# Handing the token-shifted input of the feed-forward to transfers alone, without the staging copies on GpSimd

## The reference

```python
def shift_tokens(t):
    a, s = jnp.split(t, 2, -1)
    s = jnp.pad(s, ((0, 0), (1, 0), (0, 0)))[:, :-1]
    return jnp.concatenate([a, s], -1)

for i in range(DEPTH):          # DEPTH = 6
    x = attn_layer(shift_tokens(x), Wqkv[i], q_scale[i], k_scale[i], Wo[i]) + x
    x = ffn_layer(shift_tokens(x), ln_g[i], ln_b[i], W1[i], b1[i], W2[i], b2[i]) + x
```

## Time and profile before

| | |
|---|---|
| runs of the kernel before | 6000.32, 6006.6 and 6016.27 us (median 6006.6) |
| the profiled execution | 6016.27 us, its span 6014.3 us |
| mean granted TensorE clock | 0.957 of full speed |
| PE, DVE, ACT, POOL busy | 91%, 72%, 68%, 46% of the span |
| `xs` by DMA from `staged` | 24 times, 254 KB and 1.8 KB |
| `w_qk` loads | 196 of 128 KB, median 2.1 us from issue to landing |

### The profile page before, as it was taken

One profiled execution on the slowest core, in us unless ns is written; L12 is line 12 of the kernel. 1 busy time (PEld: TensorE's weight loads), 2 busy tenths in 40 slices (PEclk: granted clock), 3 DMA queues, 4 the chain that ended last, 5 costly groups with the idle time before them and its releaser, 6 DMA issues. The chain is left out here.

```text
span 6014.3 us, 154805 instructions
## 1 busy us (share of the span) xinstructions
PE 5498.8 (91%) x57658; PEld 3896.3 (65%) x57658; DVE 4315.4 (72%) x6698; ACT 4082.8 (68%) x7766; POOL 2765.6 (46%) x2459
## 2 busy tenths in 40 slices
PE   8887996799999999999997888799999999999997
PEld 3223332677777777777776322677777778777775
DVE  7875645677777777777775886777777777777774
ACT  5774654577777777777774577577777777777774
POOL 1101100565656665556663110666556566555662
PEclk8997997899999999999999899899999999999998
DMA  0000000100000000000000000100000000000000
GB/s 12 1 1 5 2 1 9 32 18 15 18 16 15 22 15 21 14 19 16 17 20 10 4 1 1 35 16 17 18 14 19 17 16 22 14 18 16 16 20 16
DMA packets 128105, 87.16 MB, mean 14 GB/s; under 512 B 32596, under 2 KB 121200, under 8 KB 127320
## 3 DMA queue, kind: packets, MB, share of 16 engines
q1 hardware_dynamic: 127320, 76.74, 4.5%
HBM read 68.96 MB, written 1.05 MB: 12 GB/s over the span
## 5 line engine op out<-in xcount | busy, mean ns | idle before, releaser
L1742 POOL TENSOR_TENSOR cross<-raw,tab_b 128x512 f32<-128x512 f32 x768 | 999.2, 1325 | 291.7 <-ACT raw L1612 288.8
L732 DVE TENSOR_REDUCE arena<-PS 128x1 f32<-128x512 f32 (+3 forms) x1408 | 837.6, 648 | 252.5 <-PE PS L550 162.1
L1748 POOL CAST kT_b<-kT 128x512 bf16<-128x512 f32 x384 | 300.0, 781 | 1317.5 <-ACT kT L1666 1317.5
L683 ACT ACTIVATE arena<-PS 128x1024 f32<-128x1024 f32 (+1 forms) x704 | 656.4, 968 | 324.0 <-PE PS L573 238.5
L1841 DVE TENSOR_TENSOR oT<-PS,rec_den 128x288 f32<-128x288 f32 (+1 forms) x768 | 326.4, 425 | 637.2 <-ACT rec_den L1646 637.2
L1812 DVE TENSOR_TENSOR rot<-PS,tab_a 128x512 f32<-128x512 f32 x768 | 522.5, 686 | 233.0 <-PE PS L1491 142.7
L1460 PE MATMUL PS<-qT,kT 64*128 64x96 f32 x8448 | 659.3, 286 | 0.0
L1612 ACT COPY raw<-PS 128x512 f32<-128x512 f32 x768 | 448.0, 591 | 287.7 <-PE PS L1491 247.3
L1638 ACT ACTIVATE PT<-PS 128x576 f32<-128x576 f32 (+1 forms) x768 | 468.9, 611 | 254.3 <-PE PS L1460 243.3
L1828 DVE TENSOR_TENSOR rot<-rot,cross 128x1024 f32<-128x1024 f32 x384 | 611.7, 1593 | 13.3 <-POOL cross L1742 11.3
L550 PE MATMUL PS<-k_parts,q_parts 32*128 32x512 f32 (+3 forms) x1408 | 505.4, 509 | 92.7 <-DVE arena L732 78.3
(11 more groups left out here) (255 smaller groups left out, 12972.2 us busy)
## 6 DMA issues: line engine op xcount, KB each, us to landing
w_qk<-in_w_pairs SPq DMA_DIRECT2D x196, 128.0 KB, 2.1
w_v<-in_w_pairs SPq DMA_DIRECT2D x100, 128.0 KB, 2.2
w_o<-in_w_out_pairs SPq DMA_DIRECT2D x192, 64.0 KB, 1.8
xs<-staged SPq DMA_DIRECT2D x24, 254.0 KB
w<-in_L_ffn_W SPq DMA_DIRECT2D x12, 341.0 KB
q_parts<-max_rows SPq DMA_DIRECT2D x192, 2.0 KB
raw<-in_c_E SPq DMA_DIRECT2D x2, 896.0 KB, 4.5
w<-in_L_ffn_W SPq DMA_DIRECT2D x24, 64.0 KB
```

The source lines that it names most:

```text
L683: nc.scalar.activation(PT[u % 4].rearrange("p (a n) -> p a n", a=2)[:, :, first_q:512], PS[:, 2 * (u % 2):2 * (u % 2) + 2, first_q:512], A ...
L732: nc.vector.tensor_reduce(maxima[:, 2 * m + h, qt, kh:kh + 1], bank[:, 0:keys_of(qt, kh)], AX.X, ALU.max).then_inc(bank_free, 1)
L1742: nc.gpsimd.tensor_tensor(dst[:, :, :, o:o + 32], src[:, :, :, other:other + 32], tab[:, :, o:o + 32].unsqueeze(2).broadcast_to([128, 8, 2 ...
```

## The change

The POOL copies and the `staged` tile go. `xs` becomes one tile [128, 8, 128]. SP itself now waits for the two additions to x and issues three DMAs that read `x_tok` directly: the unmoved half (128 partitions, 8 pieces of 64 floats each), the moved half (127 partitions, 8 pieces of 64 floats each), and the row that wraps (7 pieces). A piece is 256 bytes. The semaphore `staged_in` goes; POOL's bias addition now waits for `xs_in`, that is, for the landing of all three. DVE reads a tile of `xs` as 128 adjacent floats instead of two runs of 64.

```diff
--- before.py
+++ after.py
@@ -1153,7 +1153,7 @@
         rec_den = [own(f"rec_den{m}", [128, 3 * QC]) for m in range(2)]
         base_a, base_b, tab_a, tab_b = (own(name, [128, BT, 128]) for name in ("base_a", "base_b", "tab_a", "tab_b"))
         scales, swapped = own("scales", [128, 128]), own("swapped", [128, 128])
-        xs, staged = own("xs", [128, 2, BT, C // 2]), own("staged", [128, BT, C // 2])
+        xs = own("xs", [128, BT, C])
         n_parts = [own(f"n_{name}", [128, N], F32R) for name in ("high", "low")]
         gated = [own(f"gated{n}", [128, N]) for n in range(3)]
         w1, w2 = own("w1", [128, 2 * INNER]), own("w2", [128, 3, C])
@@ -1195,7 +1195,7 @@
                     for z in (kT[m], qT[m], kT_b[m], qT_b[m], max_parts[m]):
                         nc.gpsimd.memset(z[:, :], 0.0).then_inc(zeroed, 1)
                 nc.gpsimd.memset(R[:, :, :], 0.0).then_inc(zeroed, 1)
-                nc.gpsimd.memset(xs[:, :, :, :], 0.0)
+                nc.gpsimd.memset(xs[:, :, :], 0.0)
                 nc.gpsimd.memset(floors[:, 0:1], -1e-24)
                 nc.gpsimd.memset(floors[:, 1:2], 65536e-24)
 
@@ -1333,11 +1333,11 @@
         with stage("full", "free0", "free1", "free2", "free3", "max_turned", "rows_made", "wqk_in", "wqk_split", "wv_in", "wv_split", "wo_in", "scales_in", "tab_a_made", "tab_b_made",
                    "st_full", "exp_done", "pv_full", "ln_done", "den_done", "o_done",
                    "raw_in", "sq_done", "red_done", "bounded", "ln2_done", "rn_ready", "cross_done", "add_done", "rot_done", "cast_done",
-                   "ff_in", "w1_split", "staged_in", "xs_in", "b2_added", "stat", "lnv", "rs", "normed", "nl_done", "xh_in", "passed") as (
+                   "ff_in", "w1_split", "xs_in", "b2_added", "stat", "lnv", "rs", "normed", "nl_done", "xh_in", "passed") as (
                 block, full, free0, free1, free2, free3, max_turned, rows_made, wqk_in, wqk_split, wv_in, wv_split, wo_in, scales_in, tab_a_made, tab_b_made,
                 st_full, exp_done, pv_full, ln_done, den_done, o_done,
                 raw_in, sq_done, red_done, bounded, ln2_done, rn_ready, cross_done, add_done, rot_done, cast_done,
-                ff_in, w1_split, staged_in, xs_in, b2_added, stat, lnv, rs, normed, nl_done, xh_in, passed):
+                ff_in, w1_split, xs_in, b2_added, stat, lnv, rs, normed, nl_done, xh_in, passed):
             free = (free0, free1, free2, free3)
 
             def filled(eng, l, b, p, name):
@@ -1392,9 +1392,12 @@
                             src = I["w_out_pairs"][bass.ds(l * PAIRS + (p - 1 + m), 1), :, :]
                             sp.dma_start(w_o[m][:, :], src.rearrange("o p n -> (o p) n")).then_inc(wo_in, 16)
                     if ff and p == 1:
-                        need(sp, staged_in, ff_index(l, b) * 2 + 2)
-                        sp.dma_start(xs[1:128, 1, :, :], staged[0:127, :, :]).then_inc(xs_in, 16)
-                        sp.dma_start(xs[0:1, 1, 1:BT, :], staged[127:128, 0:BT - 1, :]).then_inc(xs_in, 16)
+                        taken_apart(sp, l, b, 1, "Y0")
+                        taken(sp, l, b, 1, "Y1")
+                        src = x_tok[:, BT * (1 - b):BT * (1 - b) + BT, :]
+                        sp.dma_start(xs[:, :, 0:64], src[:, :, 0:64]).then_inc(xs_in, 16)
+                        sp.dma_start(xs[1:128, :, 64:128], src[0:127, :, 64:128]).then_inc(xs_in, 16)
+                        sp.dma_start(xs[0:1, 1:BT, 64:128], src[127:128, 0:BT - 1, 64:128]).then_inc(xs_in, 16)
                     if a:
                         if b == 1 and p == 1:
                             need(sp, tab_a_made, l + 1)
@@ -1763,12 +1766,6 @@
                         cross_terms(l, b, p, 1)
                         need(pool, full, fill(l, b, p, "Q3") + 1)
                         split_qk(it + 1)
-                    if ff and p == 1:
-                        taken_apart(pool, l, b, 1, "Y0")
-                        taken_apart(pool, l, b, 1, "Y1")
-                        src = x_tok[:, BT * (1 - b):BT * (1 - b) + BT, :]
-                        nc.gpsimd.tensor_copy(xs[:, 0, :, :], src[:, :, 0:64]).then_inc(staged_in, 1)
-                        nc.gpsimd.tensor_copy(staged[:, :, :], src[:, :, 64:128]).then_inc(staged_in, 1)
                     if a:
                         cast(l, b, p, 0)
                         cast(l, b, p, 1)
@@ -1788,7 +1785,7 @@
                         nc.gpsimd.tensor_tensor(w1_parts[1][:, :], w1[:, :], w1_parts[0][:, :], ALU.subtract).then_inc(w1_split, 1)
                     if ff and p == 2:
                         need(pool, ff_in, (l + b) * 96)
-                        need(pool, staged_in, phi * 2 + 2)
+                        need(pool, xs_in, phi * 48 + 48)
                         x = x_tok[:, BT * (1 - b):BT * (1 - b) + BT, :]
                         nc.gpsimd.tensor_tensor(x, x, b2_row[:, :].unsqueeze(1).broadcast_to([128, BT, C]), ALU.add).then_inc(b2_added, 1)
 
@@ -1848,9 +1845,9 @@
                 def late(l, b, p, slot):
                     phi, ff = ff_index(l, b), present(l, b, p)[4]
                     if ff and p == 2 and slot == 2:
-                        need(dve, xs_in, phi * 32 + 32)
+                        need(dve, xs_in, phi * 48 + 48)
                         for t in range(BT):
-                            nc.vector.bn_stats(stats[:, t, :], xs[:, :, t, :]).then_inc(stat, 1)
+                            nc.vector.bn_stats(stats[:, t, :], xs[:, t, :]).then_inc(stat, 1)
                     if ff and p == 2 and slot == 3:
                         need_apart(dve, stat, phi * 16 + 8)
                         for t in range(BT):
@@ -1858,7 +1855,7 @@
                     if ff and p == 3 and slot in (1, 2):
                         need(dve, rs, phi + 1)
                         for t in range(4 * slot - 4, 4 * slot):
-                            nc.vector.tensor_scalar(normed_tok[:, t, :].rearrange("p (h e) -> p h e", h=2), xs[:, :, t, :], moments[:, t, 0:1], rstd[:, t:t + 1],
+                            nc.vector.tensor_scalar(normed_tok[:, t, :], xs[:, t, :], moments[:, t, 0:1], rstd[:, t:t + 1],
                                                     ALU.subtract, ALU.mult).then_inc(normed, 1)
                     for name in late_names(l, b, p, slot):
                         kind, f = name[0], int(name[1])
```

## The result

The changed kernel takes 6053.74 us in the median (6048.82 to 6063.87, 4 runs) against 6004.14 (6000.32 to 6016.27, 4 runs): ratio 1.0085, 95% interval 1.0067 to 1.0101, about 50 us slower. The direction and the path of the loss were forecast, the size was not: 103 us were forecast, twice as much.

A forecast was written before the change was run, and what follows sets the result against it. PE, busy 91%, was taken as the bound, so stalls count only if they reach it. Tails 19, b = 1 65 and b = 0 19 make 103 us on the profiled 6016.27, 6119; forecast 6110 from the median, range 6012 to 6470.

The forecast's parts named there:

- tails: Two tails, where nothing covers DVE's wait for xs: 15.05 us becomes 24.65, +9.6 each, +19 us together.
- b = 1: Twelve places where w_qk, issued behind xs and the scale loads, reaches PE 5.4 us late: +65 us.
- the slack of `xs`: In the positions: xs, landing after 24.65 us, comes 2.3 us late for DVE at b = 1, 1.9 at b = 0.
- the time of the transfer: From DVE's addition to xs seen by DVE: 0.15 + 3.7 fixed + 20.8 for 1080 packets on one engine, 24.65 us.
- The fixed part: In the xs transfer: 3.7 us (2.9 ahead of the data, 0.8 behind) plus 0.15 for SP to notice.
- b = 0: Ten places without scale loads, where xs comes 1.9 us late for DVE and w_qk 1.5 late: +19 us.
- the landing of `w_qk` at b = 1: After SP's wrap row and eight scale loads (4.9 us), w_qk was to land 2.1 us after its issue.
- the likeliest case: The forecast itself, 19.3 ns a packet, 6110 us, chance 0.46; own range 16 ns (6045) to 24 ns (6225).
- rival 2: Descriptors made at 33 ns hold SP to the end of the xs issue; 6470 us, chance 0.17.
- rival 4: The inner 8 spreads the xs DMA over the engines, tails gain 17.5 us; 5987 us, chance 0.09.
- Rival 1: In the xs transfer a packet never costs less than one of 512 bytes, 27.8 ns; 6320 us, chance 0.15.
- Rival 3: At 12.6 ns a packet all stays hidden in the positions, only the tails lose 2.4 us each; 6012 us, chance 0.13.

The follow-up runs named there:

- the doubled transfer: Changed kernel with the moved half sent twice, the first time to a tile nobody reads; 6436.74 us, ratio 1.0717 to the kernel before.
- the cut kernel: Changed kernel with the moved half's DMA cut into two, of 112 and 15 partitions, 256-byte pieces as before; 5980.75 us, ratio 0.9958 to the kernel before.
- halves apart: Changed kernel with xs laid out in two separate halves as before, filled from x directly without copies; 6059.14 us, ratio 1.0089 to the kernel before.
- copies kept: Changed kernel with POOL's two copies kept into a tile nobody reads, SP not waiting for them; 6059.62 us, ratio 1.0075 to the kernel before.

## Why the prediction was wrong

**Right.** Which views decide; that one engine carries the shift and would carry eight times the packets; that the copies in the positions and the layout are worth nothing (`tensor_scalar` on the contiguous `xs` takes 375 ns in the mean, 379 before); that the tails lose and that the larger loss is `w_qk` at b = 1, by way of SP's held issue; the slack of `xs`, confirmed by the doubled transfer (1.0717 against 1.071 expected).

**The step that failed: the time of the transfer, 24.65 us, which came out at 20.39.** Two of its parts were too large. A packet was taken at 19.3 ns, from a line through 512 bytes of a store to memory (27.8) and 2048 bytes; it is 16.5. On 1080 packets that is 3.0 us. The fixed part was taken at 3.85 us (the 3.7 us that 127 x 79 ns left of 13.7, and 0.15); 20.39 - 1080 x 0.0165 leaves 2.6. The slack is thin, 22.4 to 22.7 us, so an error of a sixth in the transfer took away the whole term of b = 0 and almost half of the tails':
- tails +19 forecast, 10.7 measured (2 x 5.34);
- b = 0: +19 forecast, nothing measured. At 20.4 us `xs` is in time, and no wait of PE or DVE appears. POOL's wait of 4.67 us for `w_qk` there, in the first place of the loop, does not reach them;
- b = 1: +65 forecast, 34.7 measured as PE's waits (12 x 2.9 instead of 12 x 5.4).

POOL's row at that b = 0:

```profile
1500.06 1.35 POOL L1726 TENSOR_TENSOR w_qk_high<-w_qk,ones 128x256 fp32r<-128x256 f32 x1 [4.67 <-DMA w_qk<-in_w_pairs]
```

**A second step failed inside the last term, the other way: the landing of `w_qk` at b = 1, put at 2.1 us.** In the first place of the run after, SP was free 17.84 us after DVE's addition, not 22.35 (21.95 and 0.4 for the wrap row); the scales were issued in 3.85 us, not 4.9; `w_qk` was with POOL 6.5 us after its issue, not 2.1; and from there to PE's first matmul were 1.6 us, not 2.4. Together 29.7 us where 31.8 was forecast. The scale loads had been priced by their issue alone and not by their own time in the queues, although rows 7 and 8 had it: from 1306.22 to 1312.00 are 5.8 us.

That the forecast is off by no more than a factor of two is therefore partly luck. With SP's release as measured and the rest as forecast, `w_qk` would have been split 27.2 us after the addition, 0.8 us after PE wants it. Twelve times that and the tails' 10.7 make some 20 us. With 5.8 us for the landing as well, PE would have been 4.5 us late, and the same sum is 65 us. The same two terms measured 45.4.

The low end of the likeliest case's own range, computed at 16 ns, was 6045: the price of 16 ns was in the range, but the forecast took the middle. Two of the recorded sums do not follow from their own terms: rival 2 at b = 1 gives about 22 us late and not 20.5 (some 20 us more on 6470), and rival 4's 17.5 us off 6006.6 are 5989 and not 5987. Neither changes the forecast.

**The rivals.** Rival 1 (no packet under 27.8 ns) falls: 16.5 ns. The rate still drops with the size, from 26 GB/s on one engine with 2048 bytes to 16 with 256. The Trainium skill, page "DMA: Bandwidth & Descriptors", section "Specifications", wants at least 512 bytes for line rate; the trace agrees as far as 256 bytes stay below the rate of 2048, and whether the engine reads, modifies and writes there no run shows. The same page's section "Why small descriptors are slow (HBM only)" says that copies inside SBUF don't suffer; by these two rates, here they do. A line through the two sizes (16.5 and 79 ns) is, as an estimate, 8 ns a packet and 35 ns for each 1000 bytes, so about half of a small packet's time is its own price. Rival 2 (33 ns to make a descriptor) falls by the same number, and by the cut kernel, in which SP issued as many pieces in less than a microsecond a DMA. So what holds SP is not the number of pieces but their being on one engine, which fits a full queue. The hold's end, 17.8 us after the addition, lies ahead of the landing at 20.4, and the expected "until about 100 packets are left" (1.65 us at 16.5 ns) fits, if 0.8 us behind the data is right. Rival 3 is half true: b = 0 stayed hidden. Rival 4 did not occur, and the cut into 112 and 15 shows why.

**A term that was missing.** PE's matmuls are busy 16.1 us longer after, at a lower mean clock. 9.5 of these are on the matmuls that use `w_qk`, the group that starts right behind the new waits. The windows around one such wait, of 3.53 us, show the clock behind it (columns as above, PE busy first):

```profile
1324.00:1327.00 3.00, 0.04 (x1) 0.00 (x0) 0.44 (x1) 1.31 (x4) 0.92 (x2) 1.00 0.02 3
1327.00:1330.00 3.00, 2.43 (x11) 2.43 (x12) 0.06 (x1) 0.59 (x1) 3.00 (x6) 0.56 0.15 44
1330.00:1333.00 3.00, 3.00 (x47) 1.55 (x49) 1.75 (x3) 1.73 (x4) 2.92 (x3) 0.87 0.15 44
```

PE stands for 3.5 us, then the granted clock is 0.56 in the mean of 3 us, most of it at the lower level of 1.2 GHz (0.5), and the same matmuls that took 0.28 us before the wait take 0.41:

```profile
1304.37 0.28 PE L1494 MATMUL PS<-w_qk_high,x_low 128*128 128x256 f32 x1
...
1328.17 0.41 PE L1494 MATMUL PS<-w_qk_high,x_low 128*128 128x256 f32 x1
```

So this wait of PE cost more than its length. The forecast had no term for that, nor for the 9.4 us that PE waits less for DVE. The 16.1 us are a difference of two single profiles, and other kernels' profiles differ too: PE is busy 5503 to 5515 us in the three with the `w_qk` wait at b = 1 (changed, halves apart, copies kept), 5479 to 5499 in the six without it, and 5540.9 in the doubled one, where PE waits most. The price of the clock is therefore known only roughly.

## What to carry to other kernels

A DMA from partitions 0 to 126 to 1 to 127 has an outer size of 127 and ran on one engine of 16; cut into 112 and 15 partitions the wait for it was 4.6 to 4.9 us instead of 15 to 20, and this was worth more than the whole question of copies or no copies. When a transfer gets slower, price what is issued behind it too, on the issuing engine (here it was held 16 us behind 1016 pieces on one DMA engine) and in the DMA queues, by the landing times of the rows at that very place and not by a median or by issue times. Here the slack (22.4 to 22.7 us) was within a tenth of the transfer's forecast time (24.65). In such a case a forecast of the size is only as good as the price of one packet: say so in it, and give the two numbers on either side of the edge.

## What was not expected of the hardware

- Loads of 128 bytes a partition, each reading one row for all 128 partitions, landed after 4.5 to 4.9 us, and a `w_qk` load behind them after 6.3 us (5.8 before the change); issued ahead of them it was with POOL after 3.0 us. Whether the one source row or the size of the pieces makes them slow was not tried.
- With the source in pieces of 256 bytes and a destination of 2 KB side by side, no packet reached 512 bytes and the wait stayed 20.39 us.
- After a PE wait of 3.5 us, in which the granted clock stayed 1.00, it was 0.56 in the mean of the next 3 us.
